# Final stage of a fused embedding kernel: three of eight row groups are stored before the normalised rows exist, and those rows are added in memory by GpSimd's accumulating transfers

## What is computed

```python
h = concatenate([tok(x), txt(x_txt)], axis=1)          # 32 x 114 x 256
h = h + attn(layernorm(h))
h = h + ffn(layernorm(h))

def ffn(x):                                            # 8 experts, 2 of them per row
    top_vals, top_idx = top_k(x @ w_router.T, 2)
    rw = softmax(top_vals)
    h = silu(gate) * up
    y = einsum('ebsf,edf->bsed', h, w_down)
    out = sum(rw[..., None] * take_along_axis(y, top_idx[..., None], 2), 2)
    mu, var = mean(out), var(out)
    return (out - mu) * rsqrt(var + 1e-5) * ln_gamma + ln_beta
```

## Time and profile before

| | |
|---|---|
| median of 3 runs | 1217.46 us (1216.17 to 1218.94) |
| the profiled execution | 1220.45 us |
| its span, first to last instruction | 1218.6 us |
| mean granted clock of PE over the span | 0.917 |
| busy share of the span: PE, DVE, ACT, POOL | 85%, 60%, 46%, 50% |
| chain that ended last: PE, DVE, issue, POOL, DMA | 74%, 10%, 6%, 4%, 2% |

### The profile page before, as it was taken

The page is one execution under the profiler, slowest core; times in us unless marked ns, Lnnn a source line. Parts: engine busy times, 40 slices in busy tenths (PEclk is TensorE's granted clock), DMA queues, the critical chain, the costliest instruction groups (busy, mean ns, idle before and its releaser), DMA issues.

```text
span 1218.6 us, 20427 instructions
## 1 busy us (share of the span) xinstructions
PE 1041.6 (85%) x5678; PEld 827.6 (68%) x5679; DVE 727.2 (60%) x1869; ACT 559.6 (46%) x1201; POOL 607.4 (50%) x663
## 2 busy tenths in 40 slices
PE   5578998999899989997597986399999999999920
PEld 4458998999899989997354654166666666666610
DVE  2477887888688868887598797222222222222237
ACT  1335886888588857663255352022222222222224
POOL 5513675677567756776517376323333333333346
PEclk8788999999899989999799695599999999999975
DMA  9352001000100000011264342322222222223254
GB/s 265 99 147 70 2 1 62 1 2 1 61 2 1 2 9 2 10 55 57 73 223 137 108 152 61 83 41 46 43 46 45 43 43 45 46 43 47 42 137 124
DMA packets 55440, 75.42 MB, mean 62 GB/s; under 512 B 10181, under 2 KB 47683, under 8 KB 53317
## 3 DMA queue, kind: packets, MB, share of 16 engines
q1 hardware_dynamic: 32976, 48.79, 13.0%
q0 software_dynamic: 16640, 18.50, 9.2%
q10 hardware_dynamic: 5748, 7.23, 2.1%
HBM read 45.35 MB, written 29.11 MB: 61 GB/s over the span
## 4 chain that ended last, share of the span: by engine, by line
PE 74%; DVE 10%; issue 6%; POOL 4%; DMA 2%; ACT 1%; another core or an unknown queue 1%; DVEq 0%; SPq 0%; POOLq 0%; ACTq 0%
PE bank L1371 19%; PE bank L1121 16%; PE bank L1387 9%; PE bank L1186 9%; PE bank L1181 3%; PE bank L1379 2%; PE bank L1270 2%; PE bank L1083 1%; DVE arena_b L1507 1%; PE bank L1157 1%; PE bank L1149 1%; PE bank L1169 1%; PE bank L1170 1%; PE bank L1273 1%; PE bank L1362 1%
## 5 line engine op out<-in xcount | busy, mean ns | idle before, releaser
L1371 PE MATMUL bank<-arena_a,arena_b 128*128 x512 | 235.2, 602 | 0.8 <-ACT arena_b L852 0.6
L1042 POOL DMA_INDIRECT yrows<-arena_b,dest_i x64 | 99.8, 1559 | 271.5 <-ACT arena_b L864 263.9
L1507 DVE SCALAR_TENSOR_TENSOR arena_b<-bank,sml,arena_b 128x304 f32<-128x304 f32 (+2 forms) x384 | 195.4, 522 | 40.7 <-ACT arena_b L702 37.5
L1121 PE MATMUL bank<-xt_hi,w_hi 128*128 128x308 f32 x512 | 162.9, 318 | 23.0 <-POOL w_lo L923 14.4
L1825 DVE TENSOR_TENSOR arena_b<-bank,arena_b 128x512 f32<-128x512 f32 x64 | 44.2, 691 | 202.7 <-PE bank L1371 202.7
L1371 PEld LDWEIGHTS bank<-arena_a,arena_b 128*128 128x128 f32 x512 | 92.9, 191 | 99.4 <-issue 99.4
L1121 PE MATMUL bank<-xt_hi,w_lo 128*128 128x308 f32 x512 | 159.4, 311 | 0.0
L1121 PE MATMUL bank<-xt_lo,w_hi 128*128 128x308 f32 x512 | 159.0, 310 | 0.0
L945 POOL TENSOR_TENSOR u_halves<-arena_b,u_halves 128x308 fp32r<-128x308 f32 x128 | 110.5, 869 | 56.2 <-ACT arena_b L714 56.2
L939 POOL TENSOR_TENSOR y_lo<-arena_b,y_hi 128x308 fp32r<-128x308 f32 x128 | 108.5, 856 | 45.5 <-ACT y_hi L726 45.1
L1387 PE MATMUL bank<-arena_a,arena_b 128*128 x512 | 121.3, 380 | 1.1 <-DVE arena_b L1837 0.9
(11 more groups left out here) (174 smaller groups left out, 2216.6 us busy)
## 6 DMA issues: line engine op xcount, KB each, us to landing
arena_b<-xrows SPq DMA_DIRECT2D x64, 129.0 KB
arena_a<-in_w_gate SPq DMA_DIRECT2D x4, 1024.0 KB
arena_a<-in_w_up SPq DMA_DIRECT2D x4, 1024.0 KB
arena_a<-in_w_down SPq DMA_DIRECT2D x4, 1024.0 KB
yrows<-arena_b SPq DMA_DIRECT2D x1, 3648.0 KB, 18.3
h_all<-seq SPq DMA_DIRECT2D x8, 448.0 KB
arena_b<-in_patches SPq DMA_DIRECT2D x10, 324.0 KB
w_raw<-in_w_in SPq DMA_DIRECT2D x3, 1024.0 KB
```

Source lines behind the costliest of these rows:

```text
L1042: pool.indirect_dma_start(yrows, bass.IndirectOffsetOnAxis(ap=dest_i[:, k:k + 1], axis=0), f_y[k], None, compute_op=ALU.add).then_inc(y_se ...
L1121: mm = pe.matmul(out_, in_half(w, layer, d, slice(c * P, (c + 1) * P)), x[:, d, cols], start=(k == 0), stop=(k == len(pairs) - 1))
L1371: mm = pe.matmul(bank[q][:, :], x_gt[k][:, d, :], w[:, d, bass.ds(e * FFN, FFN)], start=(d == 0), stop=(d == DC - 1))
L1507: dve.scalar_tensor_tensor(acc[:, :, back_:TXT], x[:, :, 0:TXT - back_], conv_w(s // GROUPS, c, tap), acc[:, :, back_:TXT], ALU.mult, ALU. ...
```

## The change

- SP's one loop over pairs of loads becomes four loops. Between them, after the loads of pairs 8, 16 and 24, SP waits for `h2b >= 8`, `16` and `24` and stores groups 1, 3 and 5 of `h_all` (rows and bias, without the experts' output) to `out`.
- In the final stage DVE leaves out the add of groups 1, 3 and 5, and ACT leaves out their stores.
- POOL issues for these groups, after the four small instructions of groups 3, 5 and 7, two DMAs each that add the normalised rows from SBUF to the rows in `out`, and at its end waits until all six have landed.

```diff
+        h_stored, y_summed_out = sem("h_stored"), sem("y_summed_out")
+        SUMMED_BY_DMA = (1, 3, 5)
+        summed_by_dve = [g for g in range(GROUPS) if g not in SUMMED_BY_DMA]
...
-            eng.wait_ge(y_done, g + 1)
+            eng.wait_ge(y_done, summed_by_dve.index(g) + 1)
...
             load_block(0, 0)
             load_block(1, 1)
-            with sp.Fori(1, BLOCKS // 2) as pair:
-                for k in range(2):
-                    j = pair * 2 + k
-                    sp.wait_ge(f_tr, j - 1)
-                    sp.wait_ge(f_dest, j - 1)
-                    load_block(j, k)
+            first = 1
+            for last in [(g + 1) * GB + 1 for g in SUMMED_BY_DMA] + [BLOCKS // 2]:
+                with sp.Fori(first, last) as pair:
+                    for k in range(2):
+                        j = pair * 2 + k
+                        sp.wait_ge(f_tr, j - 1)
+                        sp.wait_ge(f_dest, j - 1)
+                        load_block(j, k)
+                first = last
+                if last < BLOCKS // 2:
+                    g = (last - 1) // GB - 1
+                    sp.wait_ge(h2b, (g + 1) * GB)
+                    rows = out[g * GB:(g + 1) * GB].rearrange("b s d -> s b d")
+                    for cut in CUTS:
+                        sp.dma_start(rows[cut], h_all[cut, g * GB:(g + 1) * GB, :]).then_inc(h_stored, 16)
...
-                if g % 2 == 1 and g >= 3:
-                    store_rows(act, g - 2)
             store_rows(act, GROUPS - 1)
...
                 pool.tensor_scalar(rs[:, 3, :], rs[:, 2, :], -1.0, None, ALU.mult).then_inc(y_rstd, 1)
+                if g - 2 in SUMMED_BY_DMA:
+                    done = g - 2
+                    pool.wait_ge(y_gained, done + 1)
+                    pool.wait_ge(h_stored, 16 * len(CUTS) * len(SUMMED_BY_DMA))
+                    rows = out[done * GB:(done + 1) * GB].rearrange("b s d -> s b d")
+                    for cut in CUTS:
+                        pool.dma_start(rows[cut], y_n[done][cut], accum_op=ALU.add).then_inc(y_summed_out, 16)
+            pool.wait_ge(y_summed_out, 16 * len(CUTS) * len(SUMMED_BY_DMA))
...
                 dve.wait_ge(y_normed, g + 1)
                 dve.tensor_tensor(y_n[g], y_n[g], ffn_s[0:SEQ, 0:1, :].broadcast_to([SEQ, GB, D]), ALU.mult)\
                     .then_inc(y_gained, 1)
+                if g in SUMMED_BY_DMA:
+                    return
```

More of the change, by code:

```diff
@@ L634, in _ @@
                 store_rows(sp, g)
-            sp.wait_ge(out_sent, 16 * GROUPS * len(CUTS))
+            sp.wait_ge(out_sent, 16 * len(summed_by_dve) * len(CUTS))
         @block.scalar
```

## The result

| | before | after |
|---|---|---|
| median | 1216.82 us (1213.38 to 1218.94) | 1240.26 us (1235.28 to 1241.52) |
| profiled execution | 1220.45 us | 1241.32 us |
| its span | 1218.6 us | 1239.5 us |

The ratio is 1.0188, 95% interval 1.015 to 1.0226: the change makes the kernel slower by 23.4 us. The forecast was +19.1 us and 1236.6 us.

What follows compares the result with a forecast made beforehand. The prediction took PE to bound the experts' stage and DVE to pace the final stage. Waits 10.9, queue 1.2, clock 6.0 and tail 1.0 summed to +19.1 us on 1217.5, giving 1236.6 us, range 1225 to 1246.

Steps and rivals of the forecast that it cites:

- Step 1: Experts' stage: SP's wait for the bias delays a load three times, PE standing 3.65 us each, 10.9 us in all.
- step 2: SP's queue in the experts' stage: the 448 KB store ahead of the load costs 0.4 us each, 1.2 us in all.
- Step 3: Experts' stage: PE's clock falls to half behind each of three stalls, 2.0 us each, 6.0 us in all.
- Step 4: Final stage: DVE's omitted adds bring the end forward by at most 3.4 to 4 us.
- the walk with 4.0: Final stage, POOL's pair of issues taken as 4.0 us: the last add ends at 1215.3, the old end.
- Step 5: Final stage: POOL's issue of two adding transfers costs 4.0 us, between 2.2 by DMA and 5.6 to 6.5 by row.
- Step 6: Program's end: the last accumulation lands at 1219.4, 0.8 us after the old end; the whole tail costs +1.0 us.
- Step 7: Nothing for three ACT store pairs, POOL's wait for `h_stored` and three more loop entries on SP.
- Rival A: Experts' stage: PE waits but keeps its clock, 1230.6 us; chance 0.14.
- Rival B: Final stage: POOL becomes the bound, each pair of issues costing 6.5 us, +24.6 us, 1242.1; chance 0.12.
- Rival C: Faster: the `h2b` wait is met before reaching PE and the saved adds show, -4.0 us, 1213.5; chance 0.05.
- Rival D: No effect: the load's lateness is covered and POOL eats the saved adds, 1217 to 1218 us; chance 0.03.

Runs made afterwards that it cites:

- run 5: run 3 with SP waiting at the three places for the gate product, an earlier event than the bias: 1227.69 us, ratio 1.0106.
- run 1: The changed kernel with only SP's part kept (bias waits and early stores) and the old final stage: 1229.12 us, ratio 1.018.
- run 3: The changed kernel with only SP's bias wait at the three places, the stores moved behind the last load: 1225.6 us, ratio 1.0139.
- run 2: The changed kernel with the three early stores one pair of loads later: 1208.27 us, ratio 0.9998.
- run 4: The changed kernel with its stores in place, but waiting for and reading the group of h_all one lower: 1207.98 us, ratio 1.001.
- run 6: run 2 with SP, not POOL, waiting at the end for the adding transfers: 1218.62 us, ratio 1.0018.
- run 7: run 6 with POOL issuing the adding transfers of groups 1 and 3 behind the deviations of groups 4 and 6: 1219.72 us, ratio 1.003.
- run 8: run 6 with only groups 1 and 3 added by transfers; DVE adds group 5 and ACT stores it: 1216.55 us, ratio 1.0008.

## Why the prediction was right

The direction, the place and the mechanism were as forecast. By its own steps:

- *Step 1, the wait (10.9 us) and step 2, the queue (1.2 us).* The gaps are 13.5 us against 12.1 for the two together. Step 1 was short by 0.8 to 0.95 us a place: the work between the stores and the load takes 1.80 us, not 0.89, which came from loads without a store ahead of them. Step 2's cost was not there: a load behind 448 KB takes 2.24 us. But it goes out 2.6 us after the store, not the forecast 1.6, and by then the store was nearly through (the 16 engines are 82% busy in the 1.8 us before the load's issue, 28% behind it). What 1.6 us would have cost was not measured.
- *Step 3, the clock (6.0 us)* was the mis-sized term. Behind the gaps 11.1 us were lost. Some 1.1 a place are the restart, which the prediction had left out (the table under run 5), so that about 8 us are the clock's, 2.6 a place. The half clock lasted 5.8 to 6.8 us behind the gaps, and 5.1 us behind the transpose at the stage's start, which set the upper end of 2.3.
- *Step 4, three adds.* DVE's end did come 2.8 us sooner, between the walk with 4.0 (none) and with 2.2 (4 us).
- *Step 5, POOL's issue.* 2.15 to 2.27 us for the pair, the lower end, and 1.26 to 1.42 for one, of 448 rows no more than of 8: the price goes by the DMA, not by the row. The 4.0 in the middle was wrong.
- *Step 6, the end.* +1.0 was forecast, -0.5 measured, and by another way than foreseen: the last pair needed 6.2 us from the start of its issue to its last landing, where 9.2 were forecast; the last transfer landed 3 us before the last store was through, and the drain behind it, which the prediction did not have, ended 1.1 us after that store.
- *Step 7* held but for the loop entries, whose work is part of the 1.80 us.

In sum: gaps, clock and restart, and tail make 13.5 + 11.1 - 0.5 = 24.1 us; the medians differ by 23.4. The forecast 19.1 came as near as it did with some luck: it was 7.7 us short in steps 1 and 3, and 2.7 too high in steps 2 and 6.

Rival A (clock kept) fell: it was half in all nine places of the changed kernel, run 1 and run 3. Rival B (6.5 us for a pair) fell with 2.2. Rival C is what run 2 shows once the wait is moved: its tail gain of 4 us, though, does not exist. Rival D (no change) fell with the interval.

## What to carry to other kernels

Before a wait is put into a queue of prefetches, take the spare time of the next load from the timeline (its use, less its issue, less its latency; 1.3 us here) and set it against when the awaited event comes, not against how small the added work is. The same store one pair later costs nothing. Freed time on one engine of a final stage counts only if the engine that takes over, and what it leaves to be drained, ends sooner too.

## What the runs showed of the hardware

- POOL's drain at the program's end waits for POOL's transfers. Behind POOL's own wait it takes 4.0 us (changed kernel, runs 2 to 5); begun before the last landing it takes 9.8 and 9.1 us and ends 3.6 us behind that landing (runs 6 and 7). With no such transfer late it takes 4.8 to 5.1 us and is hidden (before, runs 1 and 8).
- PE's clock can fall to half behind 1.66 us of idle and stay behind 1.88 us, in one execution (run 5); length alone does not decide. In this loop a stall cost its length, 1.1 us, and 0.40 us for each us at half clock (twelve gaps of 1.7 to 4.6 us).
- POOL issues a transfer of 448 rows of 1 KB in some 1.3 us, and DVE's two-input operations beside it do not stretch it: the last pair took 2.15 us beside a gain and an add (changed kernel, 1228.81) and 2.15 us with DVE idle for all but the last 0.3 us (run 7, 1211.61). They do stretch POOL's own arithmetic, from 1.04 to 1.99 us. The Trainium skill (SBUF — State Buffer, Who interferes with whom) tells of a probe in which `tensor_tensor` was not seen to stall DMA, and infers the reason; these rows agree with what it saw.
- Two plain stores on SP's queue put the next load off by 1.6 us, twice the 0.8 us of their issue.
